# Linear attention with memories, one core: masked queries loaded by DMA, wider score matmuls, the state copied by ScalarE, and an order of its own for each engine

## The reference

```python
q, k, v = heads(xn @ w_q.T), heads(xn @ w_k.T), heads(xn @ w_v.T)
sq, sk = elu(q) + 1, elu(k) + 1
# four memories and their sum: products with sq, each over its norm
fine = sum_m softmax_m(mean_s(sq @ norm_m)) * (sq @ mem_m) / clip(sq @ norm_m)
coarse = (sq @ sum_m mem_m) / clip(sq @ sum_m norm_m)
g = sigmoid(relu(coarse @ w1.T + b1) @ w2.T + b2)      # per token
memory = g * fine + (1 - g) * coarse
# causal linear attention; S, z: state over earlier tokens
num = (sq @ sk.T * tril) @ v + sq @ S
den = (sq @ sk.T * tril).sum(-1) + sq @ z
local = num / clip(den)
out = (gate_h * memory + (1 - gate_h) * local) @ w_o.T
```

## Time and profile before

| | |
|---|---|
| median of 3 timed runs | 671.49 us (671.04 to 671.88) |
| span of the profiled execution | 683.6 us |
| mean granted TensorE clock | 0.959 |
| attention phase | from 384.5 us to the end |
| busy: TensorE matmul, weight loads | 601.4 us (88%), 500.9 us (73%) |
| busy: VectorE, ScalarE, GpSimd | 490.6 (72%), 342.1 (50%), 287.2 us (42%) |

### The profile page before, as it was taken

How to read it: one execution, slowest core, us unless ns; L and a number is a source line. 1 busy time by engine, 2 the same in 40 slices (tenths; PEclk the granted TensorE clock), 3 DMA queues, 4 the chain that set the end, 5 groups by cost and what they waited for, 6 DMA issues and landing times. The chain is left out here.

```text
span 683.6 us, 23842 instructions
## 1 busy us (share of the span) xinstructions
PE 601.4 (88%) x8665; PEld 500.9 (73%) x8665; DVE 490.6 (72%) x1461; ACT 342.1 (50%) x870; POOL 287.2 (42%) x375
## 2 busy tenths in 40 slices
PE   1999998998995999999999588988989899889995
PEld 0787786887875899999999476766766676667773
DVE  3484565465575677777777566888888888878896
ACT  4538548548544444444444334555555555555542
POOL 2055064074072830000000303567666766666664
PEclk9999999999998899999999756999999999999997
DMA  9025535446156344445554502432443244323120
GB/s 306 34 106 200 198 138 204 164 152 217 74 199 234 113 129 154 152 150 152 156 164 128 156 23 67 131 95 66 144 142 95 66 157 130 95 66 95 34 66 32
DMA packets 62230, 88.60 MB, mean 130 GB/s; under 512 B 8532, under 2 KB 48436, under 8 KB 62132
## 3 DMA queue, kind: packets, MB, share of 16 engines
q1 hardware_dynamic: 52340, 66.61, 29.3%
q0 software_dynamic: 7520, 20.07, 9.3%
q10 hardware_dynamic: 2272, 0.53, 0.4%
HBM read 46.94 MB, written 40.24 MB: 128 GB/s over the span
## 5 line engine op out<-in xcount | busy, mean ns | idle before, releaser
L1703 POOL DMA_INDIRECT yg<-d_grouped_y,from_row x64 | 63.7, 996 | 15.5 <-issue 11.6
L986 ACT ACTIVATE silu<-e_up 128x176 f32<-128x176 f32 x72 | 22.9, 318 | 91.0 <-PE e_up L91 91.0
L89 PE MATMUL e_up<-wb,xb 128*128 x144 | 51.0, 354 | 1.5 <-DVE xb L1009 1.5
L1639 DVE TENSOR_TENSOR probs<-a_ring,causal_s 128x256 f32<-128x256 f32 x128 | 45.2, 414 | 9.3 <-PE a_ring L1400 8.9
L1545 ACT ACTIVATE hid<-a_ring,b 64x128 f32<-64x128 f32 x32 | 11.6, 363 | 79.0 <-PE a_ring L1428 75.8
L1528 ACT ACTIVATE with_mem<-a_ring 128x340 f32<-128x340 f32 x128 | 46.8, 447 | 4.5 <-PE a_ring L1381 4.5
L91 PE MATMUL e_up<-wb,xb 128*128 x144 | 46.9, 326 | 0.0
L90 PE MATMUL e_up<-wb,xb 128*128 x144 | 46.8, 325 | 0.0
L833 POOL TENSOR_TENSOR ticks<-lane 128x1 f32<-128x1 f32 x4 | 2.2, 561 | 97.7 <-DVE slot_i L746 97.7
L1418 PE MATMUL a_ring<-wo,attT 128*128 128x256 f32 x128 | 37.3, 416 | 6.5 <-ACT attT L1537 3.2
L1023 DVE TENSOR_TENSOR h_sb<-e_up,silu 128x128 f32<-128x128 f32 x72 | 21.0, 292 | 29.8 <-ACT silu L986 23.0
(11 more groups left out here) (290 smaller groups left out, 2064.6 us busy)
## 6 DMA issues: line engine op xcount, KB each, us to landing
v<-d_rows SPq DMA_DIRECT2D x77, 128.0 KB, 2.0
d_grouped_y<-y_sb SPq DMA_DIRECT2D x73, 128.0 KB, 1.9
d_v<-v_half SPq DMA_DIRECT2D x8, 544.0 KB
d_q<-halves SPq DMA_DIRECT2D x8, 512.0 KB
d_k<-halves SPq DMA_DIRECT2D x8, 512.0 KB
total<-d_base SPq DMA_DIRECT2D x8, 512.0 KB
out<-total SPq DMA_DIRECT2D x7, 512.0 KB, 3.9
v<-d_v SPq DMA_DIRECT2D x6, 544.0 KB
```

What stands on the lines that cost most here:

```text
L89: pe.matmul(out, a[0], b[0], start=start, stop=False)
L1639: dve.tensor_tensor(probs[:, j, :, :], ps[:, 0:4 * CH].rearrange("p (h i) -> p h i", i=CH), causal[:, :].unsqueeze(1).broadcast_to([P, 4, ...
L1703: pool.indirect_dma_start(yg[tile % GATHERS][:, k, :], None, d["grouped_y"], bass.IndirectOffsetOnAxis(ap=c["from"][:, k, tile:tile + 1], ...
```

## The change

Only the attention phase and what prepares it. The masked operand becomes the queries, in a buffer `masked[:, r]` that holds zeros for the other head of each pair; it is cleared once and then filled by DMAs of 16 partitions from DRAM, 16 per batch: batch 0 by GpSimd during the experts, the others by SP. The scores take the unmasked keys as weights and both masked copies of the queries as 128 moving columns. The state keeps what mixes the two heads of a pair; the product with the state uses the masked queries, one matmul for each of the two copies, so the fold is a plain copy, done by ScalarE. The state update is always written in tiles of 32 columns. coarseT and keys share a bank (turned) and a copy, hidden and gate share a bank, score products and copies of neighbouring banks are merged, tanh becomes sigmoid. Each engine has an order of its own. The first three gathers and the first base loads wait for steps of tile 0.

```diff
+def masked_parts(c, d, b, s):
+    cols = slice(s * ST, (s + 1) * ST)
+    for r in range(2):
+        for q in range(PP):
+            rows = slice(32 * q + HD * r, 32 * q + HD * (r + 1))
+            yield c["masked"][rows, r, :, cols], d["q"][b, rows, :, cols]
...
+            link(pool.memset(c["masked"][:, :, :, :], 0.0))
...
+            for h in range(NS):
+                ahead += [(*piece, c["s_mq0"][h]) for piece in masked_parts(c, d, 0, h)]
             for i, (to, source, signal) in enumerate(ahead):
-                pool.wait_ge(s_xT, 24 + 8 * i)
+                pool.wait_ge(s_xT, 24 + 2 * i)
                 pool.dma_start(to, source).then_inc(signal, 16)
...
+def tensor_order():
+    order = [("norms", 0, 0, j) for j in range(NB3)]
+    for i in range(len(TILES) + 3):
...
+            order += [("scores", *TILES[i], j) for j in range(PP)]
...
+            order.append(("oproj", *TILES[i - 3], 0))
...
+            order.append(("outT", *TILES[i - 2], 0))
...
+        order.append(("turned", b, t, 0))
+        if i + 1 < len(TILES):
+            order += [("norms", *TILES[i + 1], j) for j in range(NB3)]
+        order += [("state", b, t, 0), ("hidden", b, t, 0)]
+        if not i:
+            order.append(("mean", 0, 0, 0))
+        order += [("values", b, t, j) for j in range(2)]
+        if t < NT - 1:
+            order.append(("state", b, t, 1))
+        order.append(("local", b, t, 0))
...
+def scalar_order():
...
+            order.append(("outT", *TILES[i - 2], 0))
...
+            order.append(("turned", b, t, 0))
+            if i + 1 < len(TILES):
+                order += [("norms", *TILES[i + 1], 0), ("fold", b, t, 0), ("norms", *TILES[i + 1], 1)]
...
+            order += [("hidden", b, t, 0), ("values", b, t, 0)]
...
+            order.append(("gate", b, t, 0))
+            if t < NT - 1:
+                order.append(("fold", b, t, 1))
...
+            order.append(("rows", *TILES[i - 1], 0))
...
+def vector_order():
+    order = [("norms", 0, 0, 0), ("scores", 0, 0, 0), ("qmean", 0, 0, 0), ("norms", 0, 1, 0),
+             ("mean", 0, 0, 0), ("weights", 0, 0, 0)]
+    for i in range(1, len(TILES)):
+        order += [("local", *TILES[i - 1], 0), ("scores", *TILES[i], 0)]
+        if i > 2:
+            order.append(("oproj", *TILES[i - 3], 0))
+        order += [("coef", *TILES[i - 1], 0), ("rest", *TILES[i - 1], 0), ("fine", *TILES[i - 1], 0)]
+        if i + 1 < len(TILES):
+            order.append(("norms", *TILES[i + 1], 0))
...
+            def load_masked(b, s):
+                since(sp, ready["local"], (b - 1) * NT + (s + 1) * TS)
+                for to, source in masked_parts(c, d, b, s):
+                    sp.dma_start(to, source).then_inc(s_mq[s], 16)
...
+            sp.wait_ge(ready["scores"], 1)
             load_base(0, 0)
```

TensorE's scores:

```diff
-                                    mm = pe.matmul(to[q][h * CH:(h + 1) * CH, i * CH:(i + 1) * CH],
-                                                   masked[r][rows, m, of], sq_of[b % 2][rows, m, of],
-                                                   start=True, stop=True)
+                                mm = pe.matmul(to[q][h * CH:(h + 1) * CH, m * 2 * CH:(m + 1) * 2 * CH]
+                                               .rearrange("p (r i) -> p r i", r=2),
+                                               skT[rows, m, of], masked[rows, :, m, of], start=True, stop=True)
```

Its product with the state, in loops over the chunk `m`, the copy `r` and the half tile `h`:

```diff
+                                    mm = pe.matmul(ps[of, m * HH * VC:(m + 1) * HH * VC]
+                                                   .rearrange("p (g r e) -> p g r e", r=2, e=VC)[:, :, r, 0:HE],
+                                                   masked[:, r, m, t * P + h * CH:t * P + (h + 1) * CH],
+                                                   state[(2 * t + h) % 3][:, m, :]
+                                                   .rearrange("p (g r e) -> p g r e", r=2, e=HE)[:, :, r, :],
+                                                   start=start, stop=True, skip_group_check=not start)
```

The gate's matmul, now between that product and the transposes of `valT`:

```diff
+                    since(pe, s_hid, n + 1)
+                    pe.matmul(ring[:, place(("hidden", b, t, 0)), P:P + 1], hid[:, :], c["w2"][:, :],
+                              start=True, stop=True).then_inc(ready["gate"], 1)
```

ScalarE's fold:

```diff
+                elif what == "fold":
+                    since(act, ready["state"], b * STATES + 2 * t + j + 1)
+                    since(act, ready["local"], n)
+                    act.activation(state[(2 * t + j + 1) % 3][:, :, :].rearrange("p k n -> p (k n)"),
+                                   sums[:, 0:KC * HH * HE], ACT.Copy).then_inc(s_state, 1)
```

GpSimd's first gathers:

```diff
-                for tile in range(GATHERS):
+            for tile, signal in enumerate((ready["scores"], ready["hidden"], ready["local"])):
+                pool.wait_ge(signal, 1)
                 fetch(tile)
```

More of the change, by code:

```diff
@@ L1117, in _ @@
                       for h in range(NS)]
+            for h in range(NS):
+                ahead += [(*piece, c["s_mq0"][h]) for piece in masked_parts(c, d, 0, h)]
             for i, (to, source, signal) in enumerate(ahead):
-                pool.wait_ge(s_xT, 24 + 8 * i)
+                pool.wait_ge(s_xT, 24 + 2 * i)
                 pool.dma_start(to, source).then_inc(signal, 16)
[L1123 to L1166, removed]
+TILES = [(b, t) for b in range(B) for t in range(NT)]
 NR = 7
@@ L1172 @@
 GATHERS = 3
-NO_BANK = ("weights", "qmean", "mexp", "mask", "fine", "rest", "rows", "fold", "state", "coef")
-RING = [x for x in ATT_ORDER if x[0] not in NO_BANK]
-TURN = {use: n for n, use in enumerate(RING)}
+def tensor_order():
+    order = [("norms", 0, 0, j) for j in range(NB3)]
+    for i in range(len(TILES) + 3):
+        here = i < len(TILES)
+        if here:
+            order += [("scores", *TILES[i], j) for j in range(PP)]
+        if 0 <= i - 3 < len(TILES):
+            order.append(("oproj", *TILES[i - 3], 0))
+        if 0 <= i - 2 < len(TILES):
+            order.append(("outT", *TILES[i - 2], 0))
+        if not here:
+            continue
+        b, t = TILES[i]
+        order.append(("turned", b, t, 0))
[8 more added lines that the diff above has]
+        order.append(("local", b, t, 0))
+    return order
@@ new lines, in vector_order @@
+def vector_order():
[8 more added lines that the diff above has]
+            order.append(("norms", *TILES[i + 1], 0))
+    last = TILES[-1]
+    order += [("coef", *last, 0), ("fine", *last, 0), ("local", *last, 0), ("rest", *last, 0)]
+    return order + [("oproj", *tile, 0) for tile in TILES[-3:]]
@@ new lines, with in_pieces @@
+TENSOR_ORDER, SCALAR_ORDER, VECTOR_ORDER = tensor_order(), scalar_order(), vector_order()
+RING = [x for x in TENSOR_ORDER if x[0] != "state"]
+TURN = {use: n for n, use in enumerate(RING)}
+def in_pieces(name, b, t, most):
+    n = {"scores": PP, "norms": NB3, "values": 2}[name]
+    banks = [TURN[name, b, t, j] % NR for j in range(n)]
+    cuts = [0, *(j for j in range(1, n) if banks[j] != banks[j - 1] + 1), n]
+    if len(cuts) == 2 and n > most:
+        cuts.insert(1, n // 2)
+    return list(zip(cuts, cuts[1:]))
@@ L1178, in attention_phase, with counts_of @@
+MOST = {"scores": 4, "norms": 2, "values": 2}
+PIECES = {(name, b, t): in_pieces(name, b, t, most) for name, most in MOST.items() for b, t in TILES}
+def counts_of(name):
+    done, total = {}, 0
+    for b, t in TILES:
+        for lo, hi in PIECES[name, b, t]:
+            total += 1
+            done.update({(b, t, j): total for j in range(lo, hi)})
+    return done
+COUNT = {name: counts_of(name) for name in MOST}
 def attention_phase(nc, d, c, w):
@@ L1494, in _ @@
+                mm.then_inc(ready[what], 1)
         @block.scalar
         def _(act):
[L1496 to L1553 removed]
@@ L1733, in _, with fetch @@
-            walk(ATT_ORDER)
+            link, _ = chain(pool, s_pool)
+            def fetch(tile):
+                since(pool, s_tick, tile)
+                pool.tensor_tensor(tick_a[:, :], c["lane"][:, :], c["lane"][:, :],
+                                   ALU.add).then_inc(s_tick, 1)
+                for k in range(TOP):
+                    pool.indirect_dma_start(
+                        yg[tile % GATHERS][:, k, :], None, d["grouped_y"],
+                        bass.IndirectOffsetOnAxis(ap=c["from"][:, k, tile:tile + 1], axis=0)
+                        ).then_inc(s_ga[tile % GATHERS], 16)
@@ L1764, in build @@
         c["xg"] = [c["v1"][:, 1, :, :, :].rearrange("p t h e -> p (t h e)")[:, i * H:(i + 1) * H] for i in range(UNROLL)]
+        c["masked"] = sb("masked", [P, 2, KC, SEQ])
+        c["s_mq0"], c["s_mq"] = ([sem(f"c_{n}{h}") for h in range(NS)] for n in ("first_mq", "mq"))
         c["s_ga"] = [sem(f"c_ga{i}") for i in range(UNROLL)]
```

668 lines of the change are left out of this document (308 added, 360 removed).

## The result

The changed kernel takes 645.49 us (four runs, 641.45 to 651.39) against 671.68 us: a ratio of 0.959, interval 0.954 to 0.963. The mechanism that the forecast rests on isn't there, as the experiments show, so it is luck that the time lies in the range.

The account below looks back on a forecast made before the run. TensorE, with packed matmuls crawling under gathers, was taken to bound the tile. Tiles -8.1, opening -3.9, table load +0.3 and masks +0.5 give -11.2, so 671.49 becomes 660 us; forecast 650 to 669, range 622 to 673.

Parts of the forecast that it names:

- What bounds the kernel now: Attention's steady tile, 8.45 us: TensorE's 6.88 plus 1.28 of column-packed matmuls crawling under gathers, the rest waits on ScalarE.
- TensorE's own 6.88 us: TensorE's time per steady tile without crawl, from tile 8's 8.57 us less named waits and its wider state update.
- Steady tile after, 8.16: Attention's tile in the changed kernel: 6.88 us plus 1.28 of crawl, a gain of 8.1 us over 28 tiles.
- Scores, 0 to 0.4, taken as cancelled: TensorE's 64 score records become 32 with twice the columns: 0 to 0.4 us gain, cancelled against the state product.
- State product, up to +0.46: TensorE's product with the state goes from 8 loads to 16 of half the columns: 0 to +0.46 us.
- the second rival: Vector relief changes nothing and the state product's loads run one after the other: 670.4 us, no change; chance 0.07.
- Vector relief, nothing by itself: VectorE loses two folds, 7.22 to at most 6.35 us per tile; worth nothing while TensorE's 6.9 to 8.2 covers it.
- Opening, -3.9: Tile 0's scores lose the crawl, -6.1 us; the third gather slows tile 1's scores, +2.2; between -8 and +1.
- Table load, +0.3: Gate's tanh becomes sigmoid on ScalarE: a second table load, once, 0 to 1.3 us, at most 2.7 by the skill.
- Masks, +0.5: Masked queries by DMA: GpSimd's 22 transfers in place of 6 during the experts cost 0 to 2 us.
- The crawl goes away: Rival: gathers miss packed work or crawl has another cause; TensorE's 6.88 sets the tile, 624 us (614 to 634); chance 0.17.

Follow-up runs that it names:

- b_nogather: The kernel before, with expert rows fetched for the first three tiles only; 663.6 us, ratio 0.990.
- a_prod8: The changed kernel with the state product back in 8 records, ScalarE copying the state in two steps that zero the other head's rows; 653.52 us, ratio 0.974.
- b_open: The kernel before with the new opening alone: first three gathers and first base load wait for steps of tile 0; 670.76 us, ratio 1.001.
- b_ profiles: Profiles of edits of the kernel before, such as b_open (670.76 us) and b_nogather (663.6 us).

## Why the prediction was wrong

The step that failed is the reading under "What bounds the kernel now": that column-packed matmuls crawl at 0.11 us a record while a gather is issued, so that a tile is 6.88 us of TensorE's own work and 1.28 of crawl. Three views of the first profile agreed with it, but all three were views of one execution, 12 us over the median; a second execution shows no crawl, and without any gathers the kernel gains 7 us. What carries the result in its place is a term that the prediction took as cancelled, the scores in half as many records: 18 to 20 of the 26 us where they are added to before, 30 where they are taken from after. In the earlier trace rows the fold itself waited for TensorE 0.28 us only; the rest of its 1.6 us VectorE was on other work.

- *TensorE's own 6.88 us*: too low. It came from one tile by subtracting every named wait, but the row that gives the weight loads has TensorE's matmuls busy for 211.68 / 27.95 = 7.57 us per tile (by modelled ends), so waits that were subtracted lay beside work. In the second profile and in b_nogather tiles without a stall take about 7.5 or about 8.3 us, with gathers or without; what decides between the two is open.
- *Steady tile after, 8.16*: measured 7.30 as the median, 7.70 with the stalls.
- *Scores, 0 to 0.4, taken as cancelled*: the term that carries the result. 0.22 us per tile for the records (the middle of the range), and on top of it stalls and the halved clock behind them, of which the prediction has no term: 0.6 us per tile in all where added to before (20 / 31), 1.0 where taken from after (30 / 31).
- *State product, up to +0.46*: the 16 loads cost next to nothing; at the full clock a group keeps the engine busy 0.70 us in after and, in half as many records, 0.68 in a_prod8 (medians). The rule of the Trainium skill ("TensorE: Matmul & The Clock Gate", Part 3) isn't borne out by this pair, and the second rival falls.
- *Vector relief, nothing by itself*: 3 us on before, some 8 on after. Right in kind: it counts once TensorE is faster. The size was off: VectorE is busy 210.29 / 31 = 6.78 us per tile, not "at most" 6.35, as the coarse product now runs beside the gathers.
- *Opening, -3.9*: nothing (b_open); the 23.6 us were that execution's. Undisturbed it takes 18.9, and 17.7 after. The halved clock behind it, "left as it is", is between 14 and 34 us in all in the profiles taken, with no order by kernel.
- *Table load, +0.3*: a second load is there, once, 1.28 us at 392.84, ahead of the first gate, and none in the steady tiles.
- *Masks, +0.5*: attention begins at 377.4 us, as without them (376 to 378 in the b_ profiles; 384.5 was the first profile's own): 0.
- *The crawl goes away* (624 us): its cause was right, but 6.88 was the wrong base; the regular tile is 7.30, and with the stalls 7.70.

## What to carry to other kernels

Take a second profile of the same kernel before a theory is built on how late something is: rows that agree with each other don't count as several when one execution made them all. When an engine pauses inside a group with no semaphore to wait for, look at the instruction queue in the records of DMA packets: here many small matmuls in a row seem to use up their program faster than it comes in, and the pause costs twice where the clock falls behind it. Fewer, wider matmuls then gain more than their engine time (18 to 20 us here, where the records themselves are 7), and an order that is sparser in instructions must not give back as waits what it saves.

## What the runs showed of the hardware

TensorE's program comes in 16 KB blocks while the kernel runs, one per 5 to 6 us here. The Trainium skill ("Runtime: NRT & Kernel Launch", Instruction fetch mechanics) says the same, blocks of 256 instructions over a queue of the engine's own, and calls the cost mostly hidden; these traces agree with the block, and show 13 to 31 us of stalls in five of the six profiles with 48 or 49 blocks in attention (5 us in the first profile of before, the one that crawled). In the kernel after, the three falls of the clock in the steady stretch (425.7, 480.4, 535.0 us, each 3.4 us long at 0.5) come within 1.3 us of the end of the three longest stalls there (2.04, 2.21 and 1.92 us). Whether the next block is asked for late, and by what, the traces don't show; that the fetch is the cause rests on the timing of the gaps (212 of 215) and on the kernels with fewer instructions, not on a run that changes the fetch alone.
